# Outer products written to PSUM in pairs of words, from an operand that interleaves two time steps

## The reference

```
deltaBC = xn @ W_bc.T ; delta = softplus(deltaBC[:64] @ W_dt.T + b_dt)
Bm, Cm = the 32 + 32 other columns ; A = -exp(A_log)
for every t:   h[b,d,n] = exp(delta[b,t,d] * A[d,n]) * h[b,d,n] + (delta[b,t,d] * xn[b,t,d]) * Bm[b,t,n]
               y[b,t,d] = sum_n h[b,d,n] * Cm[b,t,n]          (then + xn * D_param, + x)
```

## Time and profile before

| | us |
|---|---|
| median of 3 runs | 1005.86 (1002.33 to 1007.05) |
| the profiled execution, its own time | 1001.59 |
| its span (first to last instruction) | 999.9 |
| TensorE busy | 873.0 (87%) |
| VectorE busy | 831.2 (83%), 570.9 of it L1606 |
| DMA | 89.93 MB in 206072 packets |

### The profile page before, as it was taken

How to read it: one execution, slowest core, us unless ns; L and a number is a source line. 1 busy time by engine, 2 the same in 40 slices (tenths; PEclk the granted TensorE clock), 3 DMA queues, 4 the chain that set the end, 5 groups by cost and what they waited for, 6 DMA issues and landing times.

```text
span 999.9 us, 22490 instructions
## 1 busy us (share of the span) xinstructions
PE 873.0 (87%) x7440; PEld 670.1 (67%) x7440; DVE 831.2 (83%) x861; ACT 460.2 (46%) x798; POOL 395.3 (40%) x737
## 2 busy tenths in 40 slices
PE   5666666159999999999999999999999969899994
PEld 3434444148777777777777777777777747787873
DVE  6655765307999999999999999999999976899884
ACT  1554444533454545544545545454545334443631
POOL 6253333412333333333333333333333544456434
PEclk9776555556999999999999999999999989999997
DMA  9399999392222222222222221222222334210101
GB/s 329 84 150 162 165 170 171 88 163 82 64 65 78 61 76 67 59 77 66 61 79 63 68 72 61 76 64 61 79 64 64 110 106 138 56 51 22 43 22 63
DMA packets 206072, 89.93 MB, mean 90 GB/s; under 512 B 139220, under 2 KB 191956, under 8 KB 205268
## 3 DMA queue, kind: packets, MB, share of 16 engines
q1 hardware_dynamic: 206036, 89.49, 38.1%
HBM read 45.85 MB, written 43.61 MB: 89 GB/s over the span
## 4 chain that ended last, share of the span: by engine, by line
PE 65%; SPq 16%; DVE 8%; POOL 4%; issue 3%; ACT 2%; DMA 1%; ACTq 0%; DVEq 0%; POOLq 0%
PE psum L1329 23%; PE psum L1298 13%; PE psum L1286 11%; PE psum L1336 9%; SPq L974 7%; SPq L1027 6%; PE psum L458 5%; POOL arena L399 2%; DVE arena L1606 2%; SPq L991 1%; POOL arena L390 1%; SPq L968 1%; PE psum L527 1%; DVE delta_mov L706 1%; ACT arena L564 1%
## 5 line engine op out<-in xcount | busy, mean ns | idle before, releaser
L1606 DVE TENSOR_TENSOR_SCAN arena<-arena,psum 128x1024 f32<-128x1024 f32 x256 | 570.9, 2274 | 48.4 <-DMA delta_terms<-arena 29.4
L1429 ACT ACTIVATE arena<-psum 128x512 f32<-128x512 f32 x512 | 278.0, 595 | 303.4 <-PE psum L1286 299.7
L1329 PEld LDWEIGHTS psum<-du_mov,b_sta 96*128 96x128 bf16 x2048 | 206.8, 131 | 130.2 <-DVE arena L1606 127.2
L1329 PE MATMUL psum<-du_mov,b_sta 96*128 96x128 bf16 x2048 | 273.0, 315 | 13.2 <-DVE arena L1606 13.1
L1180 POOL TENSOR_TENSOR carry<-arena 128x64 f32<-128x64 f32 x252 | 110.7, 439 | 357.0 <-DVE arena L1606 270.4
L1286 PE MATMUL psum<-delta_mov,a_sta 96*128 96x128 bf16 x2048 | 163.5, 224 | 8.3 <-ACT arena L1429 8.3
L1286 PEld LDWEIGHTS psum<-delta_mov,a_sta 96*128 96x128 bf16 x2048 | 144.1, 110 | 11.2 <-ACT arena L1429 10.7
L1336 PE MATMUL psum<-carry,ident 128*128 128x32 f32 x1024 | 149.2, 270 | 0.0
L1336 PEld LDWEIGHTS psum<-carry,ident 128*128 128x128 f32 x1024 | 148.4, 206 | 0.0
L1298 PE MATMUL psum<-arena,c_sta 128*32 128x512 f32 x1024 | 148.0, 643 | 0.0
L458 PE MATMUL psum<-delta_mov,arena 128*128 128x256 f32 (+6 forms) x544 | 114.6, 368 | 8.0 <-ACT arena L579 7.9
(11 more groups left out here) (142 smaller groups left out, 819.7 us busy)
## 6 DMA issues: line engine op xcount, KB each, us to landing
du_terms<-arena SPq DMA_DIRECT2D x48, 256.0 KB, 3.9
du_mov<-du_terms SPq DMA_DIRECT2D x128, 96.0 KB
y<-y_rows SPq DMA_DIRECT2D x32, 256.0 KB
b_terms<-delta_mov SPq DMA_DIRECT2D x6, 1024.0 KB, 10.6
delta_terms<-arena SPq DMA_DIRECT2D x48, 128.0 KB, 5.3
delta_mov<-delta_terms SPq DMA_DIRECT2D x128, 48.0 KB
b_sta<-b_terms SPq DMA_DIRECT2D x64, 96.0 KB
arena<-in_L_attn_x SPq DMA_DIRECT2D x8, 512.0 KB, 5.3
```

Source lines behind the costliest of these rows:

```text
L1329: mm = nc.tensor.matmul(sub(psum, 0, P, o, (4, 4), (TS, GD // 2)), b_sta[k][0:ROWS, (s * 4 + tg) * P:(s * 4 + tg + 1) * P], sub(du_mov[k], ...
L1429: nc.scalar.activation(sub(arena, 0, P, k * CHUNK_ELEMS + u * 16 * TS, (TS, 16), (D * TS, SUBS), (1, TS)), sub(psum, 0, P, (4 + u % 2) * B ...
L1606: nc.vector.tensor_tensor_scan(state[s][:, seg], decay[k][:, (s * D + g * GD) * TS:(s * D + (g + 1) * GD) * TS], psum[:, 2 * (step % 2) * ...
```

## The change

Each moving row of the outer products now holds two interleaved time steps: a row of j has its values on words 2d + (j mod 2) of each step's 512 and zeros on the others, in the side j // 2 of the buffer. So one matmul of tg writes the four steps 4tg to 4tg+3, as two pairs of neighbouring words, for 32 channels. The interleaving is made at its source: `uparts`, from which du's parts are stored, is cleared once (by POOL) and written at every second element; odd residues are loaded one element earlier, and a row of padding, stored once, stands in front. Which operand holds which parts is exchanged, so that du's rows are three plain runs of 3, 2 and 1 parts (12, 8 and 4 rows), and only 3 parts are stored, split by residue. `uparts[1]` now lies in `du_mov1`, so POOL clears that buffer once the last of its stores is done (`du_cleared`). SP's DMAs become, a tile, 12 stores of du instead of 6; a chunk, 12 loads of du instead of 4 (of twice the bytes in all) and 4 of b instead of 2. `load_md` takes the parts by a stride where it took one part several times.

```diff
 PARTS = 3
-MOVING_PART = (0, 0, 0, 1, 1, 2)
-COPIES = ((0, 3), (3, 2), (5, 1))
-STATION_PART = (0, 1, 2, 0, 1, 0)
+MOVING_PART = (0, 1, 2, 0, 1, 0)
+STATION_PART = (0, 0, 0, 1, 1, 2)
+RUNS = ((0, 3), (3, 2), (5, 1))
 ROWS = DQ * TERMS * B
 QROWS = TERMS * B
-DU_COLS = TC // 4 * D
+DU_ROW = 2 * D
+DU_SIDE = TC // 4 * DU_ROW
+DU_REGION = (L // 4 + 1) * DU_ROW
+DU_MOVES = 4 * PARTS
 BANK = 512
...
         delta_terms_d = scratch("delta_terms", [PARTS, CHUNKS, B, D, TC], BF16)
-        du_terms_d = scratch("du_terms", [TERMS, B, L, D], BF16)
+        du_terms_d = scratch("du_terms", [PARTS, B, 4, DU_REGION], BF16)
         b_terms_d = scratch("b_terms", [TERMS, B, L, P], BF16)
...
         delta_mov = [sb(f"delta_mov{k}", [P, DQ * TC * DG], BF16) for k in range(2)]
-        du_mov = [sb(f"du_mov{k}", [P, (TC // 4) * 4 * D], BF16) for k in range(2)]
+        du_mov = [sb(f"du_mov{k}", [P, 2 * DU_SIDE], BF16) for k in range(2)]
         b_sta = [sb(f"b_sta{k}", [P, (TC // 4) * P], BF16) for k in range(2)]
...
         dparts = [slot(16, 3)[:, k * 1536:(k + 1) * 1536].bitcast(BF16) for k in range(2)]
-        uparts = [slot(19, 3)[:, k * 1536:(k + 1) * 1536].bitcast(BF16) for k in range(2)]
+        uparts = [slot(19, 3).bitcast(BF16), du_mov[1][:, 0:PARTS * B * DU_ROW]]
         misc = slot(22, 2)
...
         dp_view = lambda h: dparts[h].rearrange("p (s n) -> p s n", s=3)
-        up_view = lambda h: uparts[h].rearrange("p (s n) -> p s n", s=3)
+        up_view = lambda h: uparts[h].rearrange("p (s n e) -> p s n e", s=3, e=2)[:, :, :, 0]
         bp_view = lambda h: bparts[h].rearrange("p (s n) -> p s n", s=3)
...
         MD_LOADS = DQ * PARTS
-        MU_LOADS = 4 + SUBS
+        MU_LOADS = DU_MOVES + 4
+        def load_du(eng, c, k, n):
+            j, (row, parts) = n // PARTS, RUNS[n % PARTS]
+            eng.dma_start(sub(du_mov[k], j * QROWS + row * B, parts * B, j // 2 * DU_SIDE, (1, DU_SIDE)),
+                          dram(du_terms_d, j * DU_REGION + DU_ROW - j % 2 + c * DU_SIDE,
+                               (4 * DU_REGION, parts * B), (1, DU_SIDE))).then_inc(mu_loaded[k], 16)
...
                               delta_mov[0][:, 0:row_elems]).then_inc(S["b_filled"], 16)
+            sp_.dma_start(dram(du_terms_d, 0, (DU_REGION, PARTS * B * 4), (1, DU_ROW)),
+                          delta_mov[0][0:PARTS * B * 4, 0:DU_ROW]).then_inc(S["du_padded"], 16)
...
                 for q in range(DQ):
-                    for part, (row, copies) in enumerate(COPIES):
-                        sp_.dma_start(sub(delta_mov[k], q * QROWS + row * B, copies * B, q * TC * DG, (1, TC * DG)),
-                                      dram(delta_terms_d, part * (B * L * D) + q * DG * TC + c * (B * TC * D),
-                                           (0, copies), (TC * D, B), (1, TC * DG))).then_inc(md_loaded[k], 16)
+                    for row, parts in RUNS:
+                        sp_.dma_start(sub(delta_mov[k], q * QROWS + row * B, parts * B, q * TC * DG, (1, TC * DG)),
+                                      dram(delta_terms_d, q * DG * TC + c * (B * TC * D),
+                                           (B * L * D, parts), (TC * D, B), (1, TC * DG))).then_inc(md_loaded[k], 16)
+            def load_b(c, k):
+                for j in range(4):
+                    sp_.dma_start(sub(b_sta[k], j * QROWS, QROWS, 0, (P, TC // 4), (1, P)),
+                                  dram(b_terms_d, j * P + c * (TC * P), (L * P, QROWS), (4 * P, TC // 4),
+                                       (1, P))).then_inc(mu_loaded[k], 16)
...
             def load_mu(c, k):
-                for j in range(4):
-                    sp_.dma_start(sub(du_mov[k], j * QROWS, QROWS, j * DU_COLS, (4 * D, SUBS), (1, 4 * D)),
-                                  dram(du_terms_d, j * 4 * D + c * (TC * D), (L * D, QROWS), (TS * D, SUBS),
-                                       (1, 4 * D))).then_inc(mu_loaded[k], 16)
-                for s in range(SUBS):
-                    sp_.dma_start(sub(b_sta[k], 0, ROWS, s * 4 * P, (1, 4 * P)),
-                                  dram(b_terms_d, s * TS * P + c * (TC * P), (4 * P, 4), (L * P, QROWS),
-                                       (1, 4 * P))).then_inc(mu_loaded[k], 16)
+                for n in range(DU_MOVES):
+                    load_du(sp_, c, k, n)
+                load_b(c, k)
...
                     sp_.wait_ge(S["zeros_ready"], 3)
+                    sp_.wait_ge(S["du_padded"], 16)
                     load_mu(0, 0)
...
                 sp_.wait_ge(S["ulo_ready"], lt + 1)
-                store_terms(du_terms_d, B * L * D,
-                            lambda p: up_view(k)[:, p].rearrange("p (b d) -> p b d", b=B),
-                            lt * (P * D), ((D, P), (L * D, B), (1, D)), MOVING_PART, du_stored[k])
+                for part in range(PARTS):
+                    for j in range(4):
+                        sp_.dma_start(dram(du_terms_d, (part * B * 4 + j) * DU_REGION + (1 + lt * (P // 4)) * DU_ROW,
+                                           (DU_ROW, P // 4), (4 * DU_REGION, B), (1, DU_ROW)),
+                                      sub(uparts[k], j, P // 4, part * B * DU_ROW, (DU_ROW, B), (1, DU_ROW), pstep=4))\
+                            .then_inc(du_stored[k], 16)
...
-            sp_.wait_ge(S["zeros_ready"], 4)
+            sp_.wait_ge(S["du_cleared"], 1)
             load_mu(1, 1)
...
                 rstds(1, 1)
+                for k in range(2):
+                    pool.memset(uparts[k].bitcast(F32), 0.0).then_inc(S["up_zeroed"], 1)
                 bases(0, 0, 0)
...
                 pool.memset(c_sta[k][:, :], 0.0).then_inc(S["c_sta_zeroed"], 1)
+            pool.wait_ge(du_stored[1], 16 * DU_MOVES * PAIRS)
+            pool.memset(du_mov[1][:, :].bitcast(F32), 0.0).then_inc(S["du_cleared"], 1)
             pool.wait_ge(S["c_sta_zeroed"], 2)
...
                                     d0 = g * GD + half * (GD // 2)
-                                    o = (pair_bank + half) * BANK + tg
+                                    o = (pair_bank + half) * BANK + 4 * tg
                                     mm = nc.tensor.matmul(
-                                        sub(psum, 0, P, o, (4, 4), (TS, GD // 2)),
+                                        sub(psum, 0, P, o, (2, 2), (TS, GD // 2), (1, 2)),
                                         b_sta[k][0:ROWS, (s * 4 + tg) * P:(s * 4 + tg + 1) * P],
-                                        sub(du_mov[k], 0, ROWS, (s * 4 + tg) * D + d0, (DU_COLS, 4), (1, GD // 2)),
+                                        sub(du_mov[k], 0, ROWS, (s * 4 + tg) * DU_ROW + 2 * d0, (DU_SIDE, 2), (1, GD)),
                                         start=True, stop=True)
...
             zero(delta_mov[0])
-            ZERO_AT = {3: du_mov[0], 2: delta_mov[1], 1: du_mov[1]}
+            ZERO_AT = {3: du_mov[0], 2: delta_mov[1]}
             def statistics(lt, k):
...
                     normalise(lt + 2, k, 2)
+                if seen == 0:
+                    dve.wait_ge(S["up_zeroed"], 2)
                 nc.vector.tensor_copy(up_view(k)[:, 0], du[k]).then_inc(S["uhi_ready"], 1)
...
```

More of the change, by code:

```diff
@@ L134, in build @@
             bhi_ready bres_ready bmid_ready blo_ready xd_ready base_ready half_ready args_ready exp_done
-            b_ready carry_ready decay_reset scan_done contract_done cpad_ready y_evac fw_loaded
+            b_ready carry_ready decay_reset scan_done contract_done cpad_ready du_padded du_cleared up_zeroed y_evac fw_loaded
             rd_ready wvT_psum wvT_ready wvd_psum wvd_ready tables_ready f_turned f_turn
@@ L929, in p_done @@
                 eng.wait_ge(delta_stored[k], 16 * 2 * PARTS * PAIRS)
-                eng.wait_ge(du_stored[k], 16 * TERMS * PAIRS)
+                eng.wait_ge(du_stored[k], 16 * DU_MOVES * PAIRS)
                 eng.wait_ge(base_stored[k], 16 * PAIRS)
@@ L1567, in step @@
                     normalise(lt + 2, k, 2)
+                if seen == 0:
+                    dve.wait_ge(S["up_zeroed"], 2)
                 if seen == 2:
-                    dve.wait_ge(du_stored[k], 16 * TERMS * before(lt, k))
+                    dve.wait_ge(du_stored[k], 16 * DU_MOVES * before(lt, k))
                 nc.vector.tensor_copy(up_view(k)[:, 0], du[k]).then_inc(S["uhi_ready"], 1)
@@ L1589, in _ @@
                 dve.wait_ge(delta_stored[k], 16 * 2 * PARTS * PAIRS)
-            dve.wait_ge(du_stored[0], 16 * TERMS * PAIRS)
+            dve.wait_ge(du_stored[0], 16 * DU_MOVES * PAIRS)
             def m_pair(it, first, last):
```

## The result

The kernel after takes 1059.3 us, the median of four runs (1047.2 to 1068.9), against 1004.1 for the kernel before beside it. The ratio is 1.046, with a 95% interval of 1.038 to 1.054. The forecast was 1019 us in a range of 1003 to 1038: slower was right, the size was not, and the time lies outside the range.

A forecast was written before the change was run, and what follows sets the result against it. Preparation was taken as bound by SP's issue and transfers, the main stage by VectorE's scans, with TensorE nearly as full. 1001.6 + 13.7 - 3.2 + 5 + 0.5 = 1017.6, plus 1.4: 1019 us, range 1003 to 1038.

The forecast's parts named there:

- Step 5: Preparation: 12 du stores of 128 KB a tile for 6 of 256 KB, same bytes; +0.5 us in all.
- Step 3: Way into the main stage: longer first loads, then POOL's wait and clearing before the carries; first scan +13.7 us.
- Step 6: POOL's clearing of uparts before the first base is hidden in SP's idle time; the padding DMA costs 0.5 us.
- Step 4: TensorE at low clock after the first scan: a group takes 2.4 us, if the clock rises as now; -3.2 us.
- Step 2: Main stage: SP's issues take 18.44 us a chunk against 18.27 now, so SP sets the chunk; +5 us.
- SP fits: Rival, 25%: SP's issues take 17.9 us a chunk, VectorE's 18.04 sets it; 1007 us, about no change.
- Step 1: Main stage: eight outer products fall from 0.84 to 0.45 us; VectorE's gap of 0.23 a chunk allows at most 6.7 us.

The follow-up runs named there:

- the first experiment: Against the kernel after: du stored by time step, 3 stores a tile from 128 partitions in place of 12 from 32, loads in 1 KB pieces; median 1100.9 us.

## Why the prediction was wrong, point by point

**Step 5, stores in preparation: a term taken at +0.5 us that measured about +21.** It said 12 x 0.40 = 4.8 us a tile "if free of the transfers" and +0.5 in all; measured 12 x 0.71 = 8.5. The stores alone grew by 8 x 3.4 = 27 us, of which the other issues gave back about 1.1 a tile (base and x 0.6, delta 0.3, b 0.2). The 0.40 came from other forms of DMA. The bound of 10.3 was in the text, yet the range per tile was cut to -2 and +1, on the belief that bytes set this stage. For the du stores that belief is refuted, by the landing in 2.1 us and by 3.1 us for the same bytes in three DMAs; for the issues behind them a part of it holds, as the first experiment shows. With the 2.3 us that a tile grew by (21.9 - 19.6), 8 tiles and the same other terms, the forecast would have been 1019 + 18 = 1037. Along the whole queue it is a little more: the last du issue ends 23.4 us later than before (247.62 against 224.20), of which the first loads have 2.7 and the stores 20.7.

**Step 3, the way in: right, a little high.** Of the +13.7, 3.6 was for the longer first loads, which took 2.7 more. The other 10.1 compare with 9.0 (the clearing alone, in the kernel before) and 10.3 (taken out of after); in the kernel after itself the first scan moved by 8.5 against the end of the last du issue. So +31.9 is 20.7 for the stores, 2.7 for the loads and 8.5 for the way in. The first experiment won more than the 20.7, 26.5, as its three stores cost less than the six of before. With stores and clearing both undone the first scan is at 223.70, 0.9 us from before (in the four other kernels with the same preparation at 218.5 to 230.2, so this is good to some 6 us). Step 6 was right too: the first delta store is issued at 52.22 us, before at 52.16.

**Step 4, TensorE at low clock: the condition failed, and this was the largest miss (24.6 us).** A group at low clock without contraction is 2.5 us (304.72 to 307.20 below, TensorE in time, after), as forecast 2.4. But "if the clock rises as late as now" was not so:

```profile
302.86 1.94 PE L1318 MATMUL psum<-arena,c_sta 128*32 128x512 f32 x8
304.72 1.03 PE L1349 MATMUL psum<-du_mov,b_sta 96*128 96x128 bf16 x8
...
307.20 0.53 PE L1349 MATMUL psum<-du_mov,b_sta 96*128 96x128 bf16 x3
```

With the contraction, every second group is 1.94 us longer, so two scans take 7.0 us instead of 4.6. The forecast's group of 2.4 us left it out. From 254.71 to 341.46 there are 26 scans; at 2.28 us, before's pace, that is 59.3, a loss of 27.5 us, against 6.1 before. Forecast -3.2, measured +21.4; the bound was +3. More TensorE work at the same preparation ended the phase after 20 and 28 us (all products twice, pairs apart); the wait in front of it did not lengthen it (the clearing alone).

**Step 2, SP's issues: who waits was right, the sign of the term wrong.** SP paces the chunk and TensorE waits for `delta_mov`, as the forecast said; but a chunk is 18.0 us, not 18.44: delta takes 8.56 instead of 8.95, b 1.8 instead of 2.0, and the waits less than 0.4. Outside the first low phase 230 scans take 517.6 us, 2.25 each, against 2.28 before: 6.9 us gained where 5 lost were forecast. That is the size of the rival "SP fits", got while SP doesn't fit.

**Step 1: right on TensorE, wrong on VectorE.** 0.46 us for eight products as forecast. "No speedup of TensorE can take more than 0.23 us from a chunk" was wrong. It read the length of a scan as the least distance between scans, though it is measured to the end. 99.6% busy at 2.20 and 98.7% at 2.26 look alike in a busy share.

**The sum.** Stores +20.7 (forecast +0.5), loads and way in +11.2 (+13.7), low phase +21.4 (-3.2), rest of the main stage -6.9 (+5), last stage +4.1 (low clock from 846 to 877 us, not forecast): +50.5, where +16.0 was forecast. "Slower" came out right by step 3 and, for the larger part, by two terms that the forecast had near nothing or on the other side. The median of the runs lies 7 us above the profiled execution's own time of 1052.1; the granted clock over the span was 0.824 and 0.830 in the two longest runs, 0.851 and 0.858 in the two shortest.

**What stays open.** That waits for late DMAs can bring the clock down is shown, above all with b back on SP. In the kernel after itself this costs little, two falls of 4 us; its large loss is the phase of 86 us, and what ends a low phase isn't shown. In kernels whose groups have 8 slow, 12 or 16 products the phases in the main stage last 7 to 28 us; with 8 fast ones they last 4 to 86, in the same TensorE code: 16 us after the first scan in the first experiment, 86 in the kernel after, each with TensorE's row full. One execution of the kernel before with late clearing took 1424.8 us at a mean clock of 0.55, so even slow products don't always end it.

## What to carry to other kernels

Price a DMA by the form it has, not by the bytes or by the mean of its neighbours: where the trace has no row of that form, keep the dearest row as the bound, and multiply by the number on the path. Before an engine is made faster, ask what is late when it waits: with work taken from TensorE, a late DMA became TensorE's own gap, and in several of these kernels the clock fell behind it. And read the pace of an engine as start to start in the stretch where its inputs are surely early; duration and busy share overstate it.

## What the runs showed of the hardware

- Issue time on SP's queue: 0.71 us for a store of 128 KB from 32 partitions in steps of four (landing 2.1 us after its issue), against 1.03 us for one of 512 KB from 128 partitions (landing 5.0). The same base DMA takes SP 0.54 us behind the former and 1.26 behind the latter.
- A matmul of 128 columns in bf16 costs 0.057 us into pairs 16 words apart and 0.10 us into the same words in an order in which neighbours don't follow each other.
- Scans of 128x1024 follow each other at 2.20 us and last 2.26.
- At 1.2 GHz TensorE can be busy without a gap in its row for 86 us before its clock rises.
